# Self attention on Trainium2: the probability-times-v products move to the head of the next unit on TensorE

## The reference

```python
q = einsum('bpd,hde->bphe', x, W_Q) + b_Q      # k and v likewise
q, k = rotary(q), rotary(k)
scores = where(causal, q @ k.T / sqrt(128), 0)
w = sign(scores) * exp(abs(scores) - max(abs(scores)))
attn = w / (sum(abs(w)) + 1e-6)
z = attn @ v
out = einsum('bqhd,hdm->bqm', z, W_O) + b_O
x = layernorm(x + out)
```

## Time and profile before

| what | us |
|---|---|
| runs, median of 3 | 1413.44 (1412.28 to 1413.69) |
| the profiled execution | 1414.66 |
| its span, first to last instruction | 1412.8 |
| TensorE busy | 1372.9 (97%) |
| VectorE busy | 1182.2 (84%) |
| ScalarE busy | 799.4 (57%) |
| GpSimd busy | 656.0 (46%) |

### The profile page before, as it was taken

One profiled execution on the slowest core, in us unless ns is written; L12 is line 12 of the kernel. 1 busy time (PEld: TensorE's weight loads), 2 busy tenths in 40 slices (PEclk: granted clock), 3 DMA queues, 4 the chain that ended last, 5 costly groups with the idle time before them and its releaser, 6 DMA issues.

```text
span 1412.8 us, 25497 instructions
## 1 busy us (share of the span) xinstructions
PE 1372.9 (97%) x8628; PEld 1089.1 (77%) x8642; DVE 1182.2 (84%) x1967; ACT 799.4 (57%) x1856; POOL 656.0 (46%) x748
## 2 busy tenths in 40 slices
PE   7999999999999999999999999999999999897897
PEld 6888888888888888888888888887777777542332
DVE  6888888888889888888887888865778889879996
ACT  6454544445454544455555555745555555667896
POOL 6534335245334444443523534652244444597763
PEclk9999999999999999999999999999999999999999
DMA  7301201011010110011112202311000002422454
GB/s 283 121 16 32 72 3 45 30 45 45 30 45 15 45 60 8 23 58 40 53 46 76 67 30 86 109 53 38 16 16 17 15 15 68 135 40 51 104 105 105
DMA packets 73318, 79.95 MB, mean 57 GB/s; under 512 B 45943, under 2 KB 46455, under 8 KB 72829
## 3 DMA queue, kind: packets, MB, share of 16 engines
q1 hardware_dynamic: 73212, 78.73, 18.5%
HBM read 59.83 MB, written 8.40 MB: 48 GB/s over the span
## 4 chain that ended last, share of the span: by engine, by line
PE 79%; issue 7%; DVE 6%; POOL 6%; DMA 1%; ACT 1%; SPq 0%; POOLq 0%; DVEq 0%
PE psum L360 16%; PE psum L362 16%; PE psum L361 16%; PE psum L1110 4%; PE psum L425 4%; PE psum L404 4%; PE psum L1111 3%; PE psum L1112 3%; PE psum L413 3%; PE psum L1204 2%; PE psum L427 2%; PE psum L402 2%; PE psum L1216 1%; PE psum L1221 1%; POOL acc L2127 1%
## 5 line engine op out<-in xcount | busy, mean ns | idle before, releaser
L866 POOL TENSOR_TENSOR qk<-rope_a,rope_b 128x512 f32<-128x512 f32 x128 | 177.1, 1384 | 495.6 <-DVE rope_b L591 495.6
L360 PE MATMUL psum<-x_hi,w_hi 128*128 128x512 f32 x512 | 209.4, 409 | 2.0 <-DVE x_lo L532 1.7
L362 PE MATMUL psum<-x_hi,w_lo 128*128 128x512 f32 x512 | 201.1, 393 | 0.0
L361 PE MATMUL psum<-x_lo,w_hi 128*128 128x512 f32 x512 | 200.2, 391 | 0.0
L591 DVE SCALAR_TENSOR_TENSOR rope_b<-psum,qk_bias,sin 64x512 f32<-64x512 f32 x256 | 192.0, 750 | 3.7
L715 ACT ACTIVATE e<-s 128x384 f32<-128x384 f32 x128 | 66.4, 518 | 208.3 <-DVE s L572 208.3
L360 PE MATMUL psum<-w_hi,x_hi 128*128 128x256 f32 x512 | 147.6, 288 | 1.2 <-DVE v L614 1.2
L362 PE MATMUL psum<-w_hi,x_lo 128*128 128x256 f32 x512 | 144.8, 283 | 0.0
L361 PE MATMUL psum<-w_lo,x_hi 128*128 128x256 f32 x512 | 144.7, 283 | 0.0
L634 DVE TENSOR_TENSOR acc<-psum,acc 128x512 f32<-128x512 f32 x128 | 88.5, 692 | 60.0 <-PE psum L362 44.0
L729 ACT ACTIVATE e<-p 128x128 f32<-128x128 f32 x128 | 39.3, 307 | 175.3 <-DVE p L600 175.3
(11 more groups left out here) (209 smaller groups left out, 3750.5 us busy)
## 6 DMA issues: line engine op xcount, KB each, us to landing
stage<-w_self_dram SPq DMA_DIRECT2D x64, 256.0 KB, 2.9
w_raw<-w_ffn_dram SPq DMA_DIRECT2D x32, 512.0 KB, 3.6
acc<-x_dram SPq DMA_DIRECT2D x4, 1024.0 KB, 6.6
w_signs<-w_sign SPq DMA_DIRECT2D x16, 256.0 KB, 2.1
xw_raw<-w_cross_dram SPq DMA_DIRECT2D x4, 1024.0 KB, 5.7
c_raw<-ctxT_dram SPq DMA_DIRECT2D x8, 512.0 KB, 3.5
w<-w_signs SPq DMA_DIRECT2D x2, 2048.0 KB, 12.1
out_dram<-yb SPq DMA_DIRECT2D x16, 256.0 KB, 2.1
```

The costliest lines, as they stand in the source:

```text
L360: pe.matmul(ps, ah, bh, start=n == 0, stop=False)
L361: pe.matmul(ps, ah, bl, start=False, stop=False)
L362: last = pe.matmul(ps, al, bh, start=False, stop=n == len(pairs) - 1)
L866: nc.gpsimd.tensor_tensor(qk[:, k % 2, which, :], rope_a[:, which, :], rope_b[:, which, :], ALU.add).then_inc(qk_ready, 1)
```

## The change

The mixes of unit t-3 are emitted at the head of slot t, ahead of the scores of unit t-1, where those of unit t-2 were emitted late in slot t. From slot 65 on, nothing is emitted at the head; the last two units' mixes stay in `drain`. `total_weights` gets a wait for both copies of pT made in slot 39, which the mixes gave before.

```diff
--- before.py
+++ after.py
@@ -429,7 +429,8 @@
                 if b == 1:
                     last.then_inc(z_mm, 1)
 
-            def total_weights():
+            def total_weights(t):
+                pe.wait_ge(pT_ready, (t - 2) * 2 + 2)
                 pe.wait_ge(w_folded, 2)
                 pe.wait_ge(w_consts, 1)
                 pe.matmul(psT[:, LW:LW + 2], ones[:], w_sum[:], start=True, stop=True).then_inc(w_meant, 1)
@@ -485,6 +486,9 @@
                 second = isinstance(t, int) and t in (1, 2)
                 if second:
                     project(t, k, 0)
+                if live(t, 3) and not (isinstance(t, int) and t > UNITS):
+                    mix(t - 3, (k - 3) % 8, 0)
+                    mix(t - 3, (k - 3) % 8, 1)
                 if live(t, 1):
                     score(t - 1, k - 1, 0)
                     score(t - 1, k - 1, 1)
@@ -505,9 +509,6 @@
                     project(t, k, 1)
                 if odd and o_live(t, k):
                     output(t, k, 1)
-                if live(t, 2):
-                    mix(t - 2, (k - 2) % 8, 0)
-                    mix(t - 2, (k - 2) % 8, 1)
                 if not odd and o_live(t, k):
                     output(t, k, 0)
                 if live(t, 0):
@@ -515,7 +516,7 @@
                 if not odd and o_live(t, k):
                     output(t, k, 1)
                 if isinstance(t, int) and i == SCALED_IN and k == 7:
-                    total_weights()
+                    total_weights(t)
 
             pe.wait_ge(w_consts, 1)
             for _ in range(WARM):
```

## The result

The changed kernel takes 1429.03 us (median of 4 runs, 1426.66 to 1430.07) against 1412.86 us, a ratio of 1.0111 with the interval 1.0097 to 1.0124. That is inside the forecast range, 3.6 us above the forecast. The profiled execution has a span of 1428.2 us, 15.4 more than before. One number further down leaves an execution out: one of the twelve of `odd_units` took 2948.81 us, for a cause that nothing here shows, and its median and ratio are those of the other eleven.

The account below looks back on a forecast made before the run. TensorE, busy 97% of the span, was taken as the bound. Held outputs +12.1, slot 64 +0.2 and slot 53 -0.3 summed to +12.0 us, 1413.44 to 1425.4 us; 8 in 10 from 1419.5 to 1431.

Parts of the forecast that it names:

- Part 1, the seams: TensorE: the same matmuls in another order, with new neighbours for the mixes, cost 0 (bounds -1 to +1 us).
- Part 2 (a) and (b): The v product's wait for the v copy and the first output's wait for z_lo stay covered: cost 0.
- Part 2 (c), the held output: Even slots: the second output comes 1.31 us sooner and waits for VectorE's add of the first: +12.1 us.
- the lateness: How far VectorE's add ends after the second output's turn: 0.17 us in slot 28, 7.3 us over thirty even slots.
- The price beside lateness: Each held output also pays 0.06 us to notice and 0.10 to refill: 0.16 per wait, 4.8 us in all.
- The rival of a whole exposed weight load: Each held output exposes a full weight load, so the held outputs cost 17.8 us, time 1431.1; chance 0.12.
- Why the add is late: VectorE's second sign product is held by GpSimd's rope add through a shared port; unheld, the add ends about 1.1 us sooner.
- Part 3, slot 64: ScalarE: z_high and a cast now follow the mixes at the head and delay TensorE's wait for pT: +0.2 us.
- Part 4, slot 53: The existing wait for pT there shortens because the new wait in slot 52 makes TensorE later: -0.3 us.
- The faster rival's condition: VectorE's late start in slot 53 hangs on the output it adds, so that wait falls by up to 1.31 us; chance 0.04.

Follow-up runs that it names:

- odd_units: Against the kernel before, only the mixes of odd units moved to the head; 1415.34 us against 1413.25, ratio 1.0012.
- after_apart: The changed kernel, with GpSimd's add of q's rope halves held until both sign products are done; 1412.51 us, ratio 0.9993 to the kernel before.
- even_units: Against the kernel before, only the mixes of even units moved to the head; 1429.82 us, ratio 1.0114.
- after_add_first: The changed kernel, with VectorE's add of the first output put ahead of k's rope; 1420.09 us, ratio 1.0044 to the kernel before.
- before_apart: The kernel before, with GpSimd's add of q's rope halves held until both sign products are done; 1411.46 us against 1414.08, ratio 0.9984.

## Why the prediction was right, and where its sum was short

**Part 1, the seams: right.** Even and odd slot without a hold take 14.41 + 14.40 in `after_apart` and 14.46 + 14.35 before, 28.81 both. What looked like odd slots grown by 0.05 is only a shift between the two.

**Part 2 (a) and (b), waits that stay covered: right.** No v product waits inside the loops, and no first output waits for z_lo.

**Part 2 (c), the held output: right in place and kind, its size 1.9 us short.** Against 14.41 us the held slots are 14.80 (17 slots), 14.93 (6) and 14.94 (6), and slot 4 is 15.59 against 14.51: 17 x 0.39 + 6 x 0.52 + 6 x 0.53 + 1.08 = 14.0 us, where the sum had 12.1. The term that was mis-sized is the lateness: 421.14 - 420.90 = 0.24 us, not 0.17. Counted from the slot's scores, the output's turn comes at 420.90 - 409.19 = 11.71 us, where the sum put it at 414.21 - 402.44 = 11.77; in `after_apart`, where nothing holds it, it starts at 11.71. I subtracted 1.31 us for the mixes and kept all else; but three stretches are 0.02 us shorter each: from the scores to the end of the k projection 7.48 instead of 7.50, the first output 1.36 instead of 1.38, the v product 2.87 instead of 2.89. The add ends 0.01 later. Slots 30, 32 and 4, too, are 0.06 to 0.07 us longer than the sum had them. The price beside lateness came out as the sum had it: 421.19 - 421.14 = 0.05 to notice, and 0.34 instead of 0.23 to the second matmul. The rival of a whole exposed weight load is ruled out by that.

**Why the add is late: right.** The sign product's 1.1 us beside GpSimd is shown by `after_apart`.

**Part 3, slot 64: right.** ScalarE's timeline of the changed kernel, which answers to the earlier trace rows:

```profile
937.65 0.59 ACT L744 CAST z_hi<-psum 128x512 fp32r<-128x512 f32 x1 [3.04 <-PE psum L427]
938.13 1.05 ACT L1470 CAST c_hi<-c_raw 128x1024 fp32r<-128x1024 f32 x1
939.09 0.52 ACT L716 ACTIVATE e<-s 128x384 f32<-128x384 f32 x1
```

The three now stand without idle time between them, and TensorE's wait for pT there is 1.26 instead of 1.09 us, +0.17 for a forecast of +0.2.

**Part 4, slot 53: right.** 16.05 instead of 16.45 us, -0.4 for -0.3. The faster rival's condition is refuted: VectorE's pause there is 5.04 us in the changed kernel and 5.06 before, though the output that the add waits for ends 1.3 us sooner against the scores.

**What the sum did not have.** Of the 15.4 us in the profiled executions, 14.0 - 0.4 are the loops and slot 4. From slot 64's scores to the end it is 490.75 against 489.49 us, +1.3, of which 0.2 is Part 3. Another 0.68 is idle time of TensorE in front of the first cross attention matmul, without a releaser. It stands, 0.67 to 0.71 long, in the profiled executions of all six kernels in which mixes moved, in `odd_units` and `even_units` too, and in none of the four in which they did not: it belongs to the change, the sum put it at nothing, and its cause stays open. The rest of that stretch and +0.5 ahead of the first scores are of the size by which executions of one kernel differ (its four runs span 3.4 us); I tested neither.

## What to carry to other kernels

On a saturated engine a block of work is also a distance: it keeps whatever stands behind it away from what that waits for. Before moving one, list the waits behind its old place and subtract its length from each one's spare time; here 1.14 us of spare and a block of 1.3 gave 0.39 us in every second slot, and 0.5 where the spare time was smaller. And where a chain on another engine turns out just too long, look for what stretches it; here one wait on GpSimd took away the whole loss, and the other place of the add only a part of it.

## What the runs showed that I had not expected

A short operation can be held as long as a long one: total_e, two elements a row, took 1.07 us beside GpSimd's rope add and 0.15 alone.

VectorE's pause at a taken turn of a loop is about constant from its own last instruction: 2.88 to 3.23 us in slots 13, 21 and 29 of all ten profiled executions, 4.1 to 6.4 in slot 53, and no such pause where a loop is left (slots 37 and 61). The Trainium skill ("Runtime: NRT & Kernel Launch", Instruction fetch mechanics) says that a taken branch to a target outside the fetched pages waits for a fetch. The traces agree: each of the forty pauses holds exactly one packet of the DMA queue that the profile calls "q14 instruction" (8192 bytes), and VectorE starts 1.97 to 2.13 us after that packet's start, once 2.48. In slots 13, 21 and 29 the packet starts 0.9 to 1.2 us after VectorE's last instruction, with no data packet in the pause; in slot 53 it starts 1.6 to 4.4 us after it, with 470 to 753 data packets in the pause (the loads of weights, DMA share 0.95 and 1.01 in the kernel before). So slot 53's longer pause is a later fetch, and it goes together with the loads; that the loads delay it no run here tests.

A wait of 1.79 us on TensorE was harmless to its clock in slot 53 of the kernel before, and in `after_add_first`, where the wait was 2.30 us and TensorE was busy 1.79 of 4 us, the granted clock then fell to its lower level. Part of a wait's price can lie behind it. The same wait need not cost the same in each execution, either: TensorE waits 2.75 us for pT in slot 2 of all ten profiled executions, and in eight of them its clock then falls, in those of `before_apart` and `after_apart` not. Busy time by stretch, the kernel before and then `before_apart`, TensorE first, the granted clock third from the end:

```profile
36.00:38.00 2.00, 2.00 (x7) 1.54 (x6) 0.00 (x0) 0.86 (x3) 2.00 (x2) 0.50 0.44 54
```

```profile
36.00:38.00 2.00, 2.00 (x12) 1.69 (x11) 0.45 (x1) 0.86 (x3) 2.00 (x2) 1.00 0.37 105
```

Slot 2 is 13.4 to 13.5 us long in the eight, and 11.91 and 11.95 in the two. Whether that is chance or hangs on the edit no run here tells.
